# Expert units of the first six batches, run in turn with the last batch's remaining work

## The chip, the cores and the metric

The kernel runs on one core of a Trainium2 chip. The metric is the device time of one execution in microseconds (us). Its engines are TensorE (PE, matmuls), VectorE (DVE), ScalarE (ACT), GpSimd (POOL) and SyncE (SP). POOL and SP issue the transfers of the part in question: POOL the indirect ones, that is scatters and accumulating scatters, SP the plain ones and the transposing ones.

## The reference, cut to what matters

```python
x = x + tanh(g_xattn) * attention(layernorm(x), ctx)        # x: 8 batches x 512 tokens x 512; 8 heads of 64
h = layernorm(x)
logits = h @ gate_w                                        # 8 experts
topv, topi = top_k(logits, 2);  w = softmax(topv)
Y[e] = (silu(h @ Wu[e]) * (h @ Wv[e])) @ Wo[e]             # 512 -> 128 -> 512
x = x + tanh(g_ffn) * sum_k w[k] * Y[topi[k]]
```

There are 4096 tokens with two experts each, so 8192 rows are to be added to the output. On the reference's own inputs the eight experts get 1147, 971, 688, 1113, 1074, 929, 1219 and 1051 rows; after the first six batches it is 848, 753, 417, 770, 821, 688, 1021 and 826.

## The kernel before

**Steps.** The attention goes in 32 steps `g` (batch `b`, pair of heads `j`), each `step(b, j)` being written out in program order on every engine. Tiles of 128 tokens lag behind: in step `g` PE transposes and projects the attention output of tile `n = g - 4` (`("oT", n)`, `("out", n)`), DVE adds it to the residual (`x2_rows`, L874 to L879, with the row's statistics), POOL works out the layernorm factors (`factors2`, L530 to L533), ACT normalises twice (`normalise2`, L697 and L700), POOL splits off the low half (`row_lo`, L542), SP turns the row with a transposing transfer (`turn`, L392), PE forms the logits two steps later. After a batch's four tiles DVE picks the two experts (`best_two`), PE counts ranks, DVE works out each row's place in its expert's list (`places`, done at L945), and POOL scatters the rows into the lists in device memory (`scatter`, L551, two halves of four transfers, each after a small `hold`, L518).

**The tail.** After step 31 a loop over `g = 32 .. 38` does what the last batch still needs: tiles 28 to 31, the logits of 26 to 31, the choices and scatters of batches 6 and 7.

**The table.** Then `unit_table` (DVE, L967 to L1011) cuts the lists into 39 units of 256 rows. An expert's first unit is the ragged last window of its list, pulled back so that it ends with the list (`block_ == 0`); then come blocks 1, 2, ... from the start. The pulled-back window overlaps the last whole block. Rows that would be added twice get weight 0. Units left over repeat the last expert's windows with weight 0.

**The units.** For unit `s` SP loads 256 rows (L497, three buffers), PE transposes them (L1371), multiplies by `Wu` and `Wv` (L1379) and, one unit later, by `Wo` (`down`, L1390); ACT takes tanh (L793), copies the high half (L798) and scales the two result tiles (`results`, L787, four buffers); DVE multiplies (L1147, L1153) and splits (L1157). POOL adds the results to the output with two accumulating indirect transfers of 128 rows (L631). Two such adds may touch the same output row when they belong to different experts or to overlapping windows, so `unit(s)` in POOL's program waits:

```python
if 0 < s < 3:
    pool.wait_ge(added[(s - 1) % 2], 2 * 16)
if s >= 3:
    before = pool.value_load(need[0:1, s:s + 1], min_val=2 * 16, max_val=32 * UNITS)
    pool.wait_ge(added[(s - 1) % 2], before)
hold()
pool.wait_ge(y_taken, K * (s + 1))
since(pool, added[s % 2], s // 2 * 2 * 16)
```

Every unit waits for the adds of unit `s - 2`. It waits for those of `s - 1` as well where `need` says so: where the expert differs from that of `s - 1`, or the window starts less than 256 rows from that of `s - 1` (L1006 to L1011). The general PSUM banks `G` hold both the tail's products and the units' transposed rows. The order on each engine is the program's; nothing is reordered at run time.

Of the kernel before, what the change touches and what calls it, by code (L numbers as in the profile page):

```python
# [11 lines left out]
P = 128  # L12
# [44 lines left out]

def bank_uses(B, TT):
# [27 lines left out]
    for g in range(steps, steps + 6):  # L86
        if g < steps + 4:
            names += [("oT", g - 4), ("out", g - 4)]
        names.append(("logits", g - 6))
        if g % 4 == 1:  # L90
            names.append(("ranks", g // 4 - 2))
# [3 lines left out]
def layer(nc, x, ctx_in, g1, wq, wk, wv, wo, bo, g2, gate_w, wu, wvf, wof, out, C):  # L95
# [18 lines left out]
    UNITS = ROWS * K // UR + E - 1  # L114
    HEAD = 8
# [16 lines left out]
    with ctx:  # L132
# [86 lines left out]
        cum = sb("cum", [P, 4, E])  # L219
# [6 lines left out]
        ue, unit_expert, unit_off, need = (take(UNITS) if k == 0 else take(UNITS).bitcast(U32) for k in range(4))  # L226
        uw = take(7 * UNITS).rearrange("p (k u) -> p k u", k=7)
        ids = take(K * UNITS).bitcast(U32).rearrange("p (u k) -> p u k", k=K)
        valid = take(K * UNITS).rearrange("p (u k) -> p u k", k=K)

        p32 = P32[:].rearrange("p t s -> p (t s)")
        cmp = p32[:, 0:E * BE].rearrange("p (e b) -> p e b", e=E)
        ucmp = p32[:, E * BE:E * BE + UNITS * E].rearrange("p (u e) -> p u e", e=E)
        ucmp2 = p32[:, E * BE + UNITS * E:E * BE + 2 * UNITS * E].rearrange("p (u e) -> p u e", e=E)
        spare = p32[:, E * BE + 2 * UNITS * E:4 * S]
# [77 lines left out]

        table_ready = sem("unit_table_ready")
        need_ready = sem("needed_adds_ready")
# [33 lines left out]
        def _(sp):  # L349
# [126 lines left out]
            for g in range(STEPS, STEPS + 5):  # L476
                if g < STEPS + 4:
                    load_residual(g - 4)
                turn(g - 5)
                if g < STEPS + 4:  # L480
                    store_x2(g - 4)

            sp.wait_ge(table_ready, 2)
            sp.wait_ge(outsider_st, E * K * 16)
            sp.wait_ge(prefix_st, 16)
            for r in range(2):
                for h in range(2):
                    sp.wait_ge(scattered[r][h], B // 2 * 2 * K * 16)

            def unit_rows(s):  # L490
                r = s % XG
                if s >= XG:
                    sp.wait_ge(m_filled, 2 * (s - XG) + 2)
                    sp.wait_ge(w_sel, s - XG + 1)
                    sp.wait_ge(ids_ready, s - XG + 1)
                first = sp.value_load(unit_off[0:1, s:s + 1], min_val=0, max_val=E * REGION - UR)
                sp.dma_start(xg_words[:, r], table[bass.ds(first, UR), :].rearrange("(p k) c -> p k c", k=K)) \  # L497
                    .then_inc(rows_ld[r], 16)

            for s in range(UNITS):  # L500
                unit_rows(s)
            for r in range(2):
                sp.wait_ge(x2_st[r], TILES // 2 * 16)
                sp.wait_ge(added[r], (UNITS + 1 - r) // 2 * 2 * 16)

        @block.gpsimd
        def _(pool):
# [95 lines left out]
            for g in range(STEPS, STEPS + 7):  # L603
                if g < STEPS + 5:
                    factors2(g - 5)
                if g < STEPS + 4:
                    add_bias(g - 4)
                if g < STEPS + 5:
                    row_lo(g - 5)
                if g % 4 == 2:  # L610
                    scatter(g // 4 - 2, 0)
                    scatter(g // 4 - 2, 1)

            for r in range(2):
                pool.wait_ge(x2_st[r], TILES // 2 * 16)

            pool.wait_ge(need_ready, 1)

            def unit(s):

                pool.wait_ge(ids_ready, s + 1)
                if 0 < s < 3:
                    pool.wait_ge(added[(s - 1) % 2], 2 * 16)
                if s >= 3:
                    before = pool.value_load(need[0:1, s:s + 1], min_val=2 * 16, max_val=32 * UNITS)
                    pool.wait_ge(added[(s - 1) % 2], before)
# [3 lines left out]
                for k in range(K):  # L630
                    nc.gpsimd.indirect_dma_start(out_rows, bass.IndirectOffsetOnAxis(ids[:, s, k:k + 1], 0),  # L631
# [3 lines left out]
            for s in range(UNITS):  # L635
                unit(s)

        @block.scalar
        def _(act):
# [129 lines left out]
            for g in range(STEPS, STEPS + 6):  # L769
                if g < STEPS + 4:  # L770
                    hi_part(("oT", g - 4), oT[0][:], 1.0)
                if g < STEPS + 5:
                    normalise2(g - 5)
                if g % 4 == 1:
                    gap_exp(g // 4 - 2)
# [15 lines left out]
            for s in range(UNITS):  # L791
                act.wait_ge(u_filled, s + 1)
# [11 lines left out]
        def _(dve):  # L804
# [156 lines left out]

            def unit_table():

                spread_e = lambda z: z.unsqueeze(1).to_broadcast([P, UNITS, E])
                spread_u = lambda z: z.unsqueeze(2).to_broadcast([P, UNITS, E])
                before, block_, limit, off, over, blocks, flag = (uw[:, k, :] for k in range(7))
# [4 lines left out]
                link(nc.vector.tensor_reduce(cum[:, 0, :], cmp, AXX, ALU.add))  # L971
                for k, d in enumerate((1, 2, 4)):
                    nc.vector.tensor_copy(cum[:, k + 1, 0:d], cum[:, k, 0:d])
                    link(nc.vector.tensor_tensor(cum[:, k + 1, d:E], cum[:, k, d:E], cum[:, k, 0:E - d], ALU.add))
                link(nc.vector.tensor_tensor(ucmp, spread_e(cum[:, 3, :]), spread_u(C["unit_no"][:]), ALU.is_le))
                nc.vector.tensor_reduce(limit, ucmp, AXX, ALU.add)
                link(nc.vector.tensor_tensor(ucmp2, ucmp, spread_e(cum[:, 0, :]), ALU.mult))
                link(nc.vector.tensor_reduce(before, ucmp2, AXX, ALU.add))
                nc.vector.tensor_scalar(ue, limit, float(E - 1), None, ALU.min)
                link(nc.vector.tensor_tensor(block_, C["unit_no"][:], before, ALU.subtract))  # L980

                nc.vector.tensor_copy(unit_expert, ue).then_inc(table_ready, 1)
                nc.vector.tensor_tensor(over, limit, ue, ALU.subtract)
                link(nc.vector.tensor_tensor(ucmp, spread_e(C["iota"][:]), spread_u(ue), ALU.is_equal))
                nc.vector.tensor_scalar(flag, block_, 0.0, None, ALU.is_equal)
                link(nc.vector.tensor_tensor(ucmp2, ucmp, spread_e(cum[:, 0, :]), ALU.mult))
                link(nc.vector.tensor_reduce(blocks, ucmp2, AXX, ALU.add))
                nc.vector.tensor_tensor(ucmp, ucmp, spread_e(nt[:, 1, :]), ALU.mult)
                link(nc.vector.tensor_tensor(blocks, blocks, flag, ALU.mult))
                nc.vector.tensor_reduce(limit, ucmp, AXX, ALU.add)  # L990
                link(nc.vector.tensor_tensor(block_, block_, blocks, ALU.add))
                link(nc.vector.tensor_scalar(block_, block_, -1.0, float(UR), ALU.add, ALU.mult))
                link(nc.vector.tensor_tensor(limit, limit, block_, ALU.min))
                link(nc.vector.scalar_tensor_tensor(out=off, in0=ue, scalar=float(REGION), in1=limit,
                                                    op0=ALU.mult, op1=ALU.add))
                nc.vector.tensor_scalar(unit_off, off, float(UR), None, ALU.add).then_inc(table_ready, 1)
                nc.vector.tensor_tensor(block_, block_, limit, ALU.subtract)

                step_ = flag[:, 0:UNITS - 1]
                link(nc.vector.tensor_tensor(step_, off[:, 1:UNITS], off[:, 0:UNITS - 1], ALU.subtract))  # L1000
# [45 lines left out]
            def step(b, j):  # L1046
# [60 lines left out]
                if g == 9:  # L1107
                    outsiders()
# [384 lines left out]
```

## Time and profile before

| | |
|---|---|
| time, median of 3 runs (lowest to highest) | 1117.78 us (1116.68 to 1119.32) |
| the profiled execution: its time, its span | 1116.96 us, 1115.2 us |
| mean granted TensorE clock | 0.933 of full speed |
| busy: PE, DVE, ACT, POOL | 903.0, 679.0, 572.3, 533.9 us |
| last scatter of batch 5 issued | 796.96 us |
| last scatter of batch 7 issued | 862.23 us |
| first row load of the units | 866.06 us |
| first and last add of the units issued | 884.66 and 1104.87 us |

Times within the span count from its start. The first 800 us are the attention, the next 70 the tail, the rest the units.

### The profile page before, as it was taken

The page shows a single profiled execution, that of the slowest core. Times are in us where ns is not written, and L with a number is a line of the kernel's source. Part 1 is how long each engine was busy: PE and PEld are TensorE (multiplying, and loading weights), DVE is VectorE, ACT ScalarE, POOL GpSimd, SP SyncE. Part 2 cuts the span into 40 slices and gives each one's busy share as a digit, 9 for nine tenths or more (in the row PEclk, how much of TensorE's full clock was granted, in tenths as well). Part 3 has the DMA queues.
Part 4 walks back from the last instruction along what each step waited for, and adds up shares of the span by engine and source line. Part 5 has one row for each costly group of instructions (what it writes and reads, how often), then busy time and mean ns, then how long its engine had stood idle before and what let it go on. Part 6 is the DMA issues. An engine that isn't in the chain of part 4 may idle for free.

```text
span 1115.2 us, 22759 instructions
## 1 busy us (share of the span) xinstructions
PE 903.0 (81%) x8210; PEld 543.6 (49%) x8210; DVE 679.0 (61%) x1596; ACT 572.3 (51%) x1023; POOL 533.9 (48%) x643
## 2 busy tenths in 40 slices
PE   1758898899899899989989989896650799798880
PEld 1314444455455555545545555453320677576660
DVE  3537777767867777776777777488335354344440
ACT  3316665666656655755655664465420365455450
POOL 5003224334447556446635744536564146566664
PEclk9978899999999999999999999899875799999995
DMA  6455573252254336227326434634453588899996
GB/s 225 163 149 175 164 232 115 67 150 71 76 171 112 77 103 187 72 67 204 97 58 183 112 87 140 201 77 118 135 157 103 141 185 180 166 198 188 195 152 83
DMA packets 124285, 154.26 MB, mean 138 GB/s; under 512 B 48272, under 2 KB 81040, under 8 KB 123792
## 3 DMA queue, kind: packets, MB, share of 16 engines
q1 hardware_dynamic: 107312, 115.40, 35.4%
q0 software_dynamic: 16864, 37.40, 17.6%
q8 instruction: 69, 1.13, 0.4%
q14 instruction: 40, 0.33, 0.1%
HBM read 62.83 MB, written 56.30 MB: 107 GB/s over the span
## 4 chain that ended last, share of the span: by engine, by line
PE 50%; DMA 13%; DVE 12%; ACT 8%; issue 8%; POOL 5%; SPq 3%; POOLq 1%; ACTq 0%; DVEq 0%
PE G L1173 25%; DMA out_dram<-V,Ph 9%; PE MX L1213 3%; PE ST L1228 3%; PE ST L1227 3%; PE G L1182 3%; PE MX L1379 2%; PE PV L1240 2%; PE PV L1242 2%; POOL out_dram L631 2%; PE PV L1244 2%; DVE mx L830 2%; SPq L365 2%; POOL expert_rows L551 1%; DVE tiles L820 1%
## 5 line engine op out<-in xcount | busy, mean ns | idle before, releaser
L663 ACT ACTIVATE P<-ST 128x512 f32<-128x512 f32 x256 | 153.1, 598 | 209.4 <-PE ST L1228 205.3
L588 POOL TENSOR_TENSOR Pl<-P,Ph 128x512 f16<-128x512 f32 x128 | 151.6, 1191 | 211.9 <-ACT Ph L666 211.5
L830 DVE TENSOR_REDUCE mx<-MX 128x1 f32<-128x512 f32 x256 | 168.1, 683 | 27.0 <-PE MX L1213 26.6
L666 ACT ACTIVATE Ph<-ST 128x512 f16<-128x512 f32 x256 | 154.1, 602 | 1.0 <-PE PV L1244 0.5
L631 POOL DMA_INDIRECT out_dram<-V,Ph x78 | 122.1, 1566 | 49.4 <-ACT V L787 31.7
L1379 PE MATMUL MX<-heads,tiles 128*128 128x256 f16 x936 | 118.1, 278 | 18.9 <-DVE heads L1127 18.1
L1240 PE MATMUL PV<-V,Ph 128*128 128x65 f16 x1024 | 113.3, 195 | 16.0 <-issue 16.0
L1240 PEld LDWEIGHTS PV<-V,Ph 128*128 128x128 f16 x1024 | 97.4, 98 | 36.5 <-issue 19.0
L1242 PE MATMUL PV<-V,Ph 128*128 128x64 f16 x1024 | 113.5, 197 | 0.0
L1244 PE MATMUL PV<-V,Pl 128*128 128x65 f16 x1024 | 113.1, 194 | 0.0
L1379 PEld LDWEIGHTS MX<-heads,tiles 128*128 x936 | 90.4, 100 | 41.3 <-issue 25.0
L1227 PE MATMUL ST<-heads 128*128 128x512 f16 x256 | 98.8, 386 | 9.9 <-DMA heads<-mrow 7.7
L1242 PEld LDWEIGHTS PV<-V,Ph 128*128 128x128 f16 x1024 | 96.8, 99 | 18.7 <-issue 1.2
L1213 PE MATMUL MX<-heads 128*128 128x512 f16 x256 | 91.9, 392 | 16.4 <-DVE mx L830 13.4
L1228 PE MATMUL ST<-heads 128*128 128x512 f16 x256 | 99.1, 387 | 0.0
L867 DVE TENSOR_TENSOR Pl<-P,Ph 128x512 f16<-128x512 f32 x128 | 97.0, 761 | 2.9 <-ACT Ph L666 2.9
L1244 PEld LDWEIGHTS PV<-V,Pl 128*128 128x128 f16 x1024 | 97.2, 101 | 0.0
L1173 PE MATMUL G<-tiles,wq_hi 128*128 128x512 f16 x256 | 79.8, 395 | 9.3 <-DVE tiles L820 9.3
L1173 PE MATMUL G<-wv_hi,tiles 128*128 128x512 f16 x256 | 83.2, 388 | 3.6 <-DVE V L851 2.1
L1173 PE MATMUL G<-tiles,wk_hi 128*128 128x512 f16 x256 | 76.3, 380 | 0.0
L538 POOL TENSOR_TENSOR second_norm<-second_norm,tgbo 128x512 f32<-128x512 f32 x32 | 42.4, 1325 | 66.0 <-DMA second_norm<-in_x_dram 66.0
L551 POOL DMA_INDIRECT expert_rows<-second_norm,pos_staged x64 | 65.2, 1020 | 17.3 <-issue 17.0
(204 smaller groups left out, 1872.0 us busy)
## 6 DMA issues: line engine op xcount, KB each, us to landing
heads<-expert_rows SPq DMA_DIRECT2D x39, 516.0 KB
tiles<-in_x_dram SPq DMA_DIRECT2D x32, 256.0 KB, 5.1
tiles<-in_ctx_dram SPq DMA_DIRECT2D x32, 256.0 KB, 5.3
heads<-q_hi SPq DMA_DIRECT2D x128, 64.0 KB, 2.0
heads<-k_hi SPq DMA_DIRECT2D x128, 64.0 KB, 2.0
second_norm<-in_x_dram SPq DMA_DIRECT2D x32, 256.0 KB, 3.0
out_dram<-second_norm SPq DMA_DIRECT2D x32, 256.0 KB, 2.3
expert_rows<-Pl SPq DMA_DIRECT2D x1, 4128.0 KB, 16.5
```

The lines of the kernel that those rows point to most:

```text
L588: nc.gpsimd.tensor_tensor(Pl[:, hh, c, :], P32[:, c, :], Ph[:, hh, c, :], ALU.subtract).then_inc(pl_pool, 1)
L631: nc.gpsimd.indirect_dma_start(out_rows, bass.IndirectOffsetOnAxis(ids[:, s, k:k + 1], 0), y_sb[:, s % YR, k, :], None, compute_op=ALU.add) \
L663: nc.scalar.activation(P32[:, c, :], ST[:, c % 2, :], ACT.Exp, scale=0.125 / SC2).then_inc(p_ready, 1)
L666: nc.scalar.activation(Ph[:, hh, c, :], ST[:, c % 2, :], ACT.Exp, scale=0.125 / SC2).then_inc(ph_ready, 1)
L830: nc.vector.tensor_reduce(out=mx[:, k // TT, k % TT:k % TT + 1], in_=MX[:, (k + odd) % 2, :], axis=AXX, op=ALU.max).then_inc(mx_taken, 1)
L1173: last = nc.tensor.matmul(out_, a, m, start=(n == 0), stop=(n == len(parts) - 1))
L1227: nc.tensor.matmul(ST[:, c % 2, :], K1[:, j, hh, cols], Q1[:, j, hh, :], start=True, stop=False)
L1228: nc.tensor.matmul(ST[:, c % 2, :], K2[:, j, hh, cols], Q2[:, j, hh, :], start=False, stop=True).then_inc(st_filled, 1)
L1240: nc.tensor.matmul(out_[:, 0:HD + 1], Ph[:, hh, c, cols], V[:, r, c, h, 0:HD + 1], start=(c == 0), stop=False)
L1242: nc.tensor.matmul(out_[:, 0:HD], Ph[:, hh, c, cols], V[:, r, c, h, HD + 1:], start=False, stop=False)
L1244: last = nc.tensor.matmul(out_[:, 0:HD + 1], Pl[:, hh, c, cols], V[:, r, c, h, 0:HD + 1], start=False, stop=(c == TT - 1))
L1379: last = nc.tensor.matmul(dst, w, uT[:, s % 2, a, c * UR:(c + 1) * UR], start=k == 0, stop=k == len(parts) - 1)
```

## The change

The 39 units are split in 17 early ones and 22 late ones. 17 is the number of whole blocks of 256 rows that six batches fill whatever the routing is: (6144 - 8 x 255) / 256, rounded up. A second table, `early_table`, is made by DVE at the end of step 30 from the list lengths that six batches give; it takes each expert's whole blocks in order until it has 17, and keeps in `used` how many of each expert it took. The late table (`unit_table`) takes what is left of each list: the ragged last window first, then the whole blocks after the `used` ones. The early units start once the last scores are done (their row buffers lie over the heads' operands) and batch 5 is scattered. The loop of the tail is gone; its parts stand in eight gaps `between(v)` in front of units 0 to 7 (on POOL: in front of the adds of unit `v - 1`, with the scatters of batches 6 and 7 in gaps 3 and 8). SP loads rows three units ahead, each after its gap. Unit 17 waits on POOL for the adds of unit 16 without asking the table.

```diff
+GAPS = 8
+def tail_uses(v, first):
+    names = []
+    if 1 <= v <= 4:
+        names.append(("out", first + v - 1))
+    if v <= 3:
+        names.append(("oT", first + v))
+    if v in (0, 1, 3, 4, 5, 6):
+        names.append(("logits", first - 2 + v if v < 2 else first - 3 + v))
+    if v in (2, 7):
+        names.append(("ranks", first // 4 - (v == 2)))
+    return names
...
+    EARLY_BATCHES = B - 2
+    EARLY = -(-(EARLY_BATCHES * S * K - E * (UR - 1)) // UR)
+    LATE = UNITS - EARLY
...
@@ block.sync
+            load_residual(TILES - TT)
+            sp.wait_ge(early_ready, 3)
+            sp.wait_ge(st_filled, STEPS * 8)
+            for r in range(2):
+                for h in range(2):
+                    sp.wait_ge(scattered[r][h], EARLY_BATCHES // 2 * 2 * K * 16)
+            for s in range(XG):
+                unit_rows(s)
             for s in range(UNITS):
-                unit_rows(s)
+                if s < GAPS:
+                    between(s)
+                if s + XG == EARLY:
+                    sp.wait_ge(table_ready, 3)
...
+                if s + XG < UNITS:
+                    unit_rows(s + XG)
@@ block.gpsimd
+            def between(v):
+                n = TILES - TT + v
+                if v == 0:
+                    factors2(n - 1)
+                if 2 <= v <= 5:
+                    factors2(n - 2)
+                if v < 4:
+                    add_bias(n)
+                if v == 0:
+                    row_lo(n - 1)
+                if 2 <= v <= 5:
+                    row_lo(n - 2)
+                if v in (3, 8):
+                    scatter(B - 2 + v // 8, 0)
+                    scatter(B - 2 + v // 8, 1)
...
+                if s and (s < 3 or s == EARLY):
+                    pool.wait_ge(added[(s - 1) % 2], ((s - 1) // 2 + 1) * 2 * 16)
+                elif s:
+                    wanted = pool.value_load(listed(e_need, l_need, s)[0:1], min_val=2 * 16, max_val=32 * UNITS)
+                    pool.wait_ge(added[(s - 1) % 2], wanted)
...
+            for v in range(UNITS + 1):
+                if v <= GAPS:
+                    between(v)
+                if v == EARLY:
+                    pool.wait_ge(table_ready, 3)
+                if v:
+                    unit_add(v - 1)
@@ block.scalar
+            def between(v):
+                n = TILES - TT + v
+                if v < 4:
+                    hi_part(("oT", n), oT[0][:], 1.0)
+                if v == 0:
+                    normalise2(n - 1)
+                if 2 <= v <= 5:
+                    normalise2(n - 2)
+                if v in (1, 6):
+                    gap_exp(B - 2 + v // 6)
@@ block.vector, unit_table
-                link(nc.vector.tensor_reduce(cum[:, 0, :], cmp, AXX, ALU.add))
+                link(nc.vector.tensor_reduce(cum[:, 4, :], cmp, AXX, ALU.add))
+                link(nc.vector.tensor_tensor(cum[:, 0, :], cum[:, 4, :], used, ALU.subtract))
...
+                link(nc.vector.tensor_tensor(ucmp2, ucmp, spread_e(used), ALU.mult))
+                nc.vector.tensor_reduce(done, ucmp2, AXX, ALU.add)
...
+                link(nc.vector.tensor_tensor(block_, block_, done, ALU.add))
@@ block.vector
+                if g == STEPS - 2:
+                    early_table()
...
+                if 1 <= v <= 4:
+                    x2_rows(n - 1)
+                if v < 4:
+                    lo_part(("oT", n), oT[1][:], oT[0][:], 1.0)
...
+                if v == 7:
+                    unit_table()
@@ block.tensor
+                if units_turned.value:
+                    pe.wait_ge(t_lo if u % 2 else t_hi, units_turned.value)
...
+                pe.wait_ge(evacuated, use["oT", TILES - TT] if s == 0 else 1 + max(
+                    use[name] for v in range(min(s, GAPS)) for name in tail_uses(v, TILES - TT)))
```

On POOL, before, the scatters of batch 7 (`expert_rows`) end the tail and the adds (`out_dram`) come behind them, each behind its `junk` hold:

```order
L518 TENSOR_TENSOR junk<-ones 128x1
L551 DMA expert_rows<-second_norm,pos_staged 34944x516 x4
L518 TENSOR_TENSOR junk<-ones 128x1
L551 DMA expert_rows<-second_norm,pos_staged 34944x516 x4
L518 TENSOR_TENSOR junk<-ones 128x1
L631 DMA out_dram<-V,Ph 4096x512 x2
L518 TENSOR_TENSOR junk<-ones 128x1
L631 DMA out_dram<-V,Ph 4096x512 x2
```

On POOL now, the end of gap 3, with the scatters of batch 6, stands between the adds of unit 1 and unit 2, and the factors of tile 30 stand behind unit 2's adds:

```order
L586 TENSOR_TENSOR second_norm<-second_norm,tgbo 128x512
L590 TENSOR_TENSOR second_norm<-second_norm 128x512
L566 TENSOR_TENSOR junk<-ones 128x1
L599 DMA expert_rows<-second_norm,pos_staged 34944x516 x4
L566 TENSOR_TENSOR junk<-ones 128x1
L599 DMA expert_rows<-second_norm,pos_staged 34944x516 x4
L566 TENSOR_TENSOR junk<-ones 128x1
L682 DMA out_dram<-V,xn 4096x512 x2
L578 TENSOR_SCALAR ln_factors<-row_mean_var 128x1
L579 TENSOR_TENSOR ln_factors<-ln_factors,ln_constants 128x1
L580 TENSOR_SCALAR ln_factors<-ln_factors 128x1
L581 TENSOR_SCALAR ln_factors<-row_mean_var,ln_factors 128x1
```

What moved: adds, scatters and the factors of the last tiles share POOL's program in turn, where before every factor and scatter stood ahead of the first add.

On DVE now, the late table (43 instructions, of which the first four and the last two are shown) stands in gap 7, between the places of batch 7 and unit 7's first product (`P<-P,MX`):

```order
L1007 CAST pos_staged<-pos_f 128x8
L1035 TENSOR_TENSOR nt<-base,list_starts 128x8
L1036 TENSOR_SCALAR nt<-nt 128x8
L1037 TENSOR_TENSOR P<-nt,block_starts 128x128
L1039 TENSOR_REDUCE cum<-P 128x8
...
L1080 TENSOR_TENSOR Ph<-Ph 128x21
L1081 SCALAR_TENSOR_TENSOR Ph<-Ph,adds_before 128x21
L1262 SCALAR_TENSOR_TENSOR P<-P,MX 128x256
L1234 COPY heads<-G 128x1024
```

Before (39 instructions), on DVE, it had the same place behind the places of batch 7, and unit 0's turned rows (`heads<-G`) came next:

```order
L945 CAST pos_staged<-pos_f 128x8
L967 TENSOR_TENSOR nt<-base,list_starts 128x8
L968 TENSOR_SCALAR nt<-nt 128x8
...
L1010 TENSOR_TENSOR Ph<-Ph 128x38
L1011 SCALAR_TENSOR_TENSOR Ph<-Ph,adds_before 128x38
L1127 COPY heads<-G 128x1024
```

What moved: the table stood ahead of all units; now seven units are ahead of it.

## Rows read from the trace of the kernel before

**Rows 1.** The page: the span, and its part on transfers issued (residual tiles)

```profile
span 1115.2 us, 22759 instructions
...
second_norm<-in_x_dram SPq DMA_DIRECT2D x32, 256.0 KB, 3.0
```

**Rows 2.** Windows: us; PE, PEld, DVE, ACT, POOL busy; clock, DMA share, GB/s

```profile
801.50:872.50 71.00, 24.15 (x219) 13.41 (x215) 27.26 (x127) 11.19 (x17) 33.20 (x47) 0.65 0.40 127
...
884.00:990.00 106.00, 97.26 (x907) 76.29 (x906) 49.78 (x176) 57.54 (x98) 57.24 (x51) 0.97 0.87 182
```

**Rows 3.** Timeline of POOL: first adds of units 0, 2, 5, 17, 31, 35, 36, 38

```profile
884.66 1.62 POOL L631 DMA_INDIRECT out_dram<-V,Ph  x1 [11.72 <-ACT V L787]
...
903.37 1.57 POOL L631 DMA_INDIRECT out_dram<-V,Ph  x1 [0.39 <-ACT V L787]
...
922.11 1.56 POOL L631 DMA_INDIRECT out_dram<-V,Ph  x1 [0.50 <-issue]
...
990.25 1.56 POOL L631 DMA_INDIRECT out_dram<-V,Ph  x1 [0.50 <-issue]
...
1069.79 1.56 POOL L631 DMA_INDIRECT out_dram<-V,Ph  x1 [0.50 <-ACT V L787]
...
1087.22 1.56 POOL L631 DMA_INDIRECT out_dram<-V,Ph  x1 [1.43 <-ACT V L787]
...
1095.13 1.56 POOL L631 DMA_INDIRECT out_dram<-V,Ph  x1 [0.50 <-issue]
...
1103.01 1.56 POOL L631 DMA_INDIRECT out_dram<-V,Ph  x1 [0.40 <-issue]
```

**Rows 4.** Waits, 866 to the end: who waited for whom, total, times, longest

```profile
POOL junk L518 <- DMA out_dram<-V,Ph: 43.0, 8, 6.5
```

**Rows 5.** Transfers that write the output: issue to landing

```profile
DMA to landing us min/median/max: 2.0/5.3/8.5
```

**Rows 6.** The chain that ended last: pieces of one unit on PE

```profile
883.54 1.31 PE MX L1379 x12
884.85 0.89 PE G L1371 x16
...
887.05 1.29 PE PV L1390 x6
```

**Rows 7.** Timeline of POOL: last scatter of batch 5; batch 6's scatter; bias

```profile
796.96 0.96 POOL L551 DMA_INDIRECT expert_rows<-second_norm,pos_staged  x1 [0.30 <-issue]
...
823.12 0.19 POOL L518 TENSOR_TENSOR junk<-ones 128x1 f32<-128x1 f32 x1
...
833.60 0.25 POOL L530 TENSOR_SCALAR ln_factors<-row_mean_var 128x1 f32<-128x1 f32 x1
...
835.15 1.27 POOL L538 TENSOR_TENSOR second_norm<-second_norm,tgbo 128x512 f32<-128x512 f32 x1
```

**Rows 8.** Timeline of SP's queue: the first five row loads

```profile
866.06 15.96 SPq L497 DMA_DIRECT2D heads<-expert_rows  x5
```

**Rows 9.** Timeline of ACT: second normalisation of tile 30; unit 1's tanh; unit 0's results

```profile
835.95 0.80 ACT L700 ACTIVATE second_norm<-second_norm,ln_factors 128x512 f16<-128x512 f32 x1
...
880.08 0.39 ACT L793 ACTIVATE P<-MX 128x256 f32<-128x256 f32 x1 [0.36 <-PE MX L1379]
...
883.14 1.25 ACT L787 ACTIVATE V<-ST,unit_scales 128x512 f32<-128x512 f32 x2
```

**Rows 10.** Timeline of DVE: first and last instruction of the table

```profile
851.98 0.16 DVE L967 TENSOR_TENSOR nt<-base,list_starts 128x8 f32<-128x8 f32 x1
...
861.71 0.20 DVE L1011 SCALAR_TENSOR_TENSOR Ph<-Ph,adds_before 128x38 uint32<-128x38 f32 x1
```

**Rows 11.** Windows of 5 us where PE idled; columns as in rows 2

```profile
970.00:975.00 5.00, 0.35 (x3) 0.24 (x3) 1.51 (x4) 2.59 (x5) 2.56 (x4) 0.82 0.81 109
975.00:980.00 5.00, 5.00 (x33) 4.02 (x32) 2.20 (x8) 2.85 (x5) 4.54 (x5) 0.50 1.05 215
...
1025.00:1030.00 5.00, 1.90 (x12) 0.87 (x10) 1.51 (x4) 2.73 (x5) 3.94 (x4) 1.00 1.05 145
```

More of the change, by code:

```diff
@@ L85, in bank_uses @@
         names += second
[L86 to L91, printed above, removed]
+    for v in range(GAPS):
+        names += tail_uses(v, steps - 4)
     return names
@@ L602, in _, with unit_add @@
                     step(b, j)
[L603 to L619, printed above, removed]
-                pool.wait_ge(ids_ready, s + 1)
[L622 to L626, printed above, removed]
+            def between(v):
[13 more added lines that the diff above has]
+                    scatter(B - 2 + v // 8, 1)
+            def unit_add(s):
+                pool.wait_ge(ids_ready, s + 1)
+                if s in (0, EARLY):
+                    for r in range(2):
+                        pool.wait_ge(x2_st[r], (EARLY_BATCHES * TT if s == 0 else TILES) // 2 * 16)
+                if s and (s < 3 or s == EARLY):
[3 more added lines that the diff above has]
+                    pool.wait_ge(added[(s - 1) % 2], wanted)
                 hold()
@@ L768, in _, with between @@
                     step(b, j)
[L769 to L775, printed above, removed]
+            def between(v):
+                n = TILES - TT + v
+                if v < 4:
+                    hi_part(("oT", n), oT[0][:], 1.0)
+                if v == 0:
+                    normalise2(n - 1)
+                if 2 <= v <= 5:
+                    normalise2(n - 2)
+                if v in (1, 6):
+                    gap_exp(B - 2 + v // 6)
             def unit_hi(s):
@@ L791, in _ @@
             for s in range(UNITS):
+                if s < GAPS:
+                    between(s)
                 act.wait_ge(u_filled, s + 1)
@@ L1145, in _ @@
             for s in range(UNITS):
+                if s < GAPS:
+                    between(s)
                 dve.wait_ge(tanh_ready, s + 1)
@@ L1162, in _ @@
         def _(pe):
+            units_turned = Count(0)
             def bank(name):
@@ L1355, in _, with between @@
             pe.wait_ge(o_ready, B * HB)
-            for g in range(STEPS, STEPS + 6):
-                if g < STEPS + 4:
-                    transposes(("oT", g - 4), O[(B - 1) % 2][:, g - STEPS, :])
-                    out_project(g - 4)
-                logits(g - 6)
-                if g % 4 == 1:
-                    ranks(g // 4 - 2)
+            def between(v):
+                for name in tail_uses(v, TILES - TT):
+                    what, n = name
+                    if what == "out":
+                        out_project(n)
+                    elif what == "oT":
+                        transposes(name, O[(B - 1) % 2][:, v, :])
+                    elif what == "logits":
+                        logits(n)
+                    else:
+                        ranks(n)
             def unit_transposes(s):
                 r = s % XG
+                units_turned.take()
                 pe.wait_ge(rows_ld[r], (s // XG + 1) * 16)
+                pe.wait_ge(evacuated, use["oT", TILES - TT] if s == 0 else 1 + max(
+                    use[name] for v in range(min(s, GAPS)) for name in tail_uses(v, TILES - TT)))
                 for a, taken in ((0, t_hi), (1, t_lo)):
@@ L1403, in _ @@
             for s in range(UNITS):
+                if s < GAPS:
+                    between(s)
                 pe.wait_ge(t_hi, s + 1)
```

190 lines of the change are left out of this document (119 added, 71 removed).

## The prediction

> **What bounds the kernel now.** I read the windows first. After the last head PE works 24.15 of 71 us up to the units, at a clock of 0.65 [rows 2]: that is the slack which the change is about. In the units PE works 97.26 of 106 us and the transfers show 0.87 [rows 2]. One unit is, on PE, 0.89 us of transposes, twice 1.31 for `Wu` and `Wv` and 1.29 for `Wo` [rows 6]: 4.8 us. But from unit 17 to unit 31, 14 units, the adds take 1069.79 - 990.25 = 79.5 us [rows 3], 5.7 us each. What takes the rest shows in the waits: eight times POOL's hold in front of an add stands until the previous unit's adds have landed, 43.0 us in all [rows 4]. With lists of 1147, 971, 688, 1113, 1074, 929, 1219 and 1051 rows the experts have 5, 4, 3, 5, 5, 4, 5 and 5 units, 36; their changes fall on units 5, 9, 12, 17, 22, 26 and 31, and unit 36, the first spare one, repeats the ragged window beside the block that it overlaps. These are eight waits, and the count agrees. Units 1 and 2 wait by the program.
>
> What such a wait costs: units 0 to 2 are two waited intervals, (903.37 - 884.66) / 2 = 9.36 us each; from unit 35 to 36, with no row load left, it is 1095.13 - 1087.22 = 7.91. An interval without it is (1103.01 - 1095.13) / 2 = 3.94, POOL's own pace [rows 3]. PE runs ahead meanwhile, by up to four result buffers, so one wait among five units costs little. Waits in a row are another matter: then a unit costs 8 to 9 us, whatever PE does.
>
> **The change, part by part.** I follow the time of the adds.
>
> *Start.* Before, 3.8 us passed from the last scatter's issue at 862.23 to the first row load at 866.06 [rows 8]. The last scatter of batch 5 is issued at 796.96 [rows 7], so the first load comes at 800.8, 65 us earlier. The first add came 884.66 - 866.06 = 18.6 us behind the load. Gaps 0 and 1 now stand in it (a projection, two turned tiles, two logits, a choice of experts), of which some 4 us are not hidden: first add near 823.5.
>
> *Early table.* Some 23 small DVE instructions; the table of before has 39 in 861.71 + 0.20 - 851.98 = 9.9 us [rows 10], so these are about 5.5 us, behind step 30. I cost them at nothing: scores and exponentials of step 31 cover them, and uncovered they cost 5.5.
>
> *Gaps 2 to 7.* Each is a round through POOL, ACT, DVE and PE. When ACT ends unit v-2's results, POOL issues their adds (3.8 us, above), then works out the factors of the next tile, on which ACT's two normalisations wait: from 833.60 [rows 7] to 835.95 + 0.80 = 836.75 [rows 9], 3.15 us for both. ACT's tanh of unit v stands behind them; from a tanh to the end of the previous unit's results it is 883.14 + 1.25 - 880.08 = 4.3 us [rows 9]. The sum is 11.2 us a round. PE's own work in it (4.8, and near 4 of projection, turning and logits) is hidden.
> - Gaps 2 and 5: 11.2 each.
> - Gaps 3 and 4: between them POOL has adds 3.8, factors and normalisation 3.15, the residual's load 3.0 [rows 1], its bias 1.27 [rows 7] and a low half of about as much, then batch 6's scatters from 823.12 to 833.60, 10.5 us [rows 7], adds 3.8, factors and normalisation 3.15, and 4.3. Sum 34.
> - Gap 6: no factors, but the last turned row and the choice of two experts; 7.5, an estimate between 4.3 and 11.2.
> - Gap 7: places (some 2 us), the late table (43 narrower instructions, 9.9 as before), then 4.3: 16.
> - Sum 80. Unit 6's adds come at 823.5 + 80 = 903.5. Batch 7's scatters stand ahead of unit 7's: + 3.8 + 10.5 = 917.8.
>
> *Early units 7 to 17.* The early list (3, 2, 1, 3, 3, 2, 3 blocks of experts 0 to 6) changes expert at 9, 12 and 14, and 17 waits always. A group of three with its wait is 922.11 - 903.37 = 18.7 us [rows 3]; one of two is a waited 9.4 and an unwaited 3.9 to 4.3, so 13.5. Unit 17: 917.8 + 13.5 + 18.7 + 13.5 + 18.7 = 982. Before it is 990.25 [rows 3]. Of a head start of 65 us, 8 are left.
>
> *Late units.* The early table took all whole blocks but the last from most lists. What is left of the eight is 2, 2, 2, 2, 2, 2, 2 and 5 units. In every pair the first is the ragged window, pulled back, the second the last whole block, which it overlaps: 891 and 768 for expert 0, 715 and 512 for expert 1, and so on, always less than 256 apart. So `need` asks for the previous adds at the change of expert and again inside the pair: all 14 intervals from unit 17 to unit 31 are waited ones, where before three were. Before, the overlapping blocks stood three to four units apart and needed nothing of this. Each interval lies between 7.91 (no row loads beside the adds) and 9.36 (nearly two loads beside each, since PE ran at 4.8). With one load beside each I take 8.7. That is 122 us in place of 79.5: unit 31 at 1104.
>
> By the Trainium skill (DMA: Bandwidth & Descriptors, "Anatomy of one DMA") a transfer costs about 2.0 us and its bytes at 436 GB/s; an add of 256 KB would be back 2.6 us after its issue. The interval would then be some 5.2 us (half of POOL's 3.94 up to the second transfer, 2.6, and the hold), and the 14 waits would cost nothing; the rows show 7.91 where the adds are alone, so I weigh it only as a rival.
>
> *End.* Unit 31 begins a group of five, as before; from there to the end 1115.2 - 1069.79 = 45.4 us [rows 1, 3] stay.
>
> Sum of the span: 1104 + 45.4 = 1149.4, 34 above 1115.2. The profiled execution took 1116.96, 1.8 above its span, and the median is 0.8 above that: 1152; with gaps that may overlap a little better than in my sum I say 1151.
>
> **Rivals.**
> 1. *The adds' waits are short when the queue is empty, and the kernel is faster.* The place is the 14 intervals from unit 17 to 31. It decides at (1069.79 - 982) / 14 = 6.3 us an interval. For it: the shortest landing of such a transfer is 2.0 us [rows 5]; then POOL's own pace of 3.94 and PE's 4.8 bound an interval, and the total 982 + 67 + 45.4 + 2.6 = 1097. Against it: the median is 5.3 [rows 5], and the interval with no load beside it is 7.91. The skill's figure above gives 5.2 an interval, so 1103. Chance 0.05.
> 2. *PE falls to its lower clock in the gaps and the late units, and becomes the bound.* After a stretch with 0.35 us of work in 5 PE's clock is 0.50 for the next 5, that is 1.2 GHz in place of 2.4; after one with 1.90 of 5 it stays at 1.00 [rows 11]. Late units leave PE 8.7 - 4.8 = 3.9 us idle each, between the two. At 1.2 GHz a unit is 9.6 us of PE, 0.9 over the interval: 13 us over 14; a gap is near 17.6 against 11.2, up to 25 over four. Half of the whole gives 1170. Chance 0.13. [...]
> 3. *The gaps cost little and the late waits alone count.* If ACT does not wait for POOL's factors, a round is some 6 us, unit 17 comes near 965 (the waited groups catch up with it in part), and the total is near 1133. Chance 0.12; against it stands ACT's program order.
> 4. *No difference:* the head start and the waits cancel. That is the band around rival 1's point. Chance 0.02.
>
> **How the numbers follow.** Forecast 0.68, rivals 0.05, 0.13, 0.12, 0.02. A measurement here can tell 0.2% (2.2 us) from nothing. Bounds of the forecast: late intervals 7.91 or 9.36, -11 or +9; gaps 10 either way. That is 1130 to 1170; the range goes a little beyond on both sides for rivals 2 and 3: 1128 to 1174. Faster 0.05, same 0.02, slower 0.93.
>
> **What would show it.** In the profile after: first add of the output near 823, unit 17's near 982; POOL's holds in front of adds waiting on the output's transfers some 20 times instead of 8, above 80 us in all; 14 intervals of 8 to 9 us from unit 17 on; PE busy about 4.8 of each, transfers' share well under 0.87 there; ACT waiting for the factors in gaps 2 to 5. I am wrong if intervals of waited adds fall under 6.3 us, or if the start of the units slips behind 830.

## The result, and the profile after

The changed kernel takes 1153.17 us (median of 4 runs, 1151.42 to 1158.87), where the kernel before takes 1118.55 us (4 runs, 1116.68 to 1121.18). The ratio is 1.0316, 95% interval 1.0289 to 1.0343: slower by 34.6 us. The forecast was 1151. The profiled execution took 1152.34 us, with a span of 1150.5. All ratios in this document compare fast runs; one execution of the kernel before, taken beside experiments 5 to 8, was slow (2078.95 us) and is left out of them.

I read the profile after in the order of the forecast's steps. First POOL's timeline, first adds of units 0, 1, 3, 6, 7, 17 and 31. The columns are start, duration, line and operation, and in brackets how long POOL had idled before it and what ended that.

```profile
823.32 1.67 POOL L682 DMA_INDIRECT out_dram<-V,xn  x1 [3.52 <-ACT V L847]
...
835.62 1.65 POOL L682 DMA_INDIRECT out_dram<-V,xn  x1 [0.18 <-issue]
...
869.66 1.66 POOL L682 DMA_INDIRECT out_dram<-V,xn  x1 [2.16 <-ACT V L847]
...
904.02 1.56 POOL L682 DMA_INDIRECT out_dram<-V,xn  x1 [5.93 <-ACT V L847]
...
918.24 1.83 POOL L682 DMA_INDIRECT out_dram<-V,xn  x1 [0.16 <-POOL junk L566]
...
982.00 1.55 POOL L682 DMA_INDIRECT out_dram<-V,Ph  x1 [0.52 <-ACT V L847]
...
1105.73 1.55 POOL L682 DMA_INDIRECT out_dram<-V,Ph  x1 [0.50 <-ACT V L847]
```

Against [rows 3] the first add comes 61.3 us earlier (823.32, before 884.66), unit 17's 8.3 us earlier (982.00, before 990.25), and unit 31's 35.9 us later (1105.73, before 1069.79). So the head start is lost in two places. From the first add to unit 17, 158.7 us pass in place of 105.6: 53 us given back, 48.6 of them up to unit 7, that is in the gaps (94.9 in place of 46.3), and 4.4 between units 7 and 17. From unit 17 to unit 31, 123.7 in place of 79.5: 44 us more than before. Behind unit 31 nothing changed: 1150.5 - 1105.73 = 44.8, before 45.4 [rows 1, 3].

The waits from 800 us to the end (who waited for whom; us in total, times, longest), the four lines that the forecast spoke of:

```profile
POOL junk L566 <- DMA out_dram<-V,Ph: 70.2, 15, 5.6
...
ACT second_norm L754 <- POOL ln_factors L581: 30.5, 4, 15.8
...
POOL junk L566 <- DMA out_dram<-V,xn: 29.3, 6, 6.2
...
ACT P L855 <- PE MX L1505: 10.3, 12, 2.1
```

POOL's hold in front of an add waits for the adds of the unit before 21 times and 99.5 us; before it was 8 times and 43.0 us [rows 4]. (`V,xn` and `V,Ph` are the same result buffers; the early and the late table lie in different memory.) ACT waits for PE's `Wu` products (`MX`), with which each unit begins on ACT, for no more than 10.3 us in all: PE is not what the late units wait for.

The windows: first the old tail's, then the gaps, the early units 7 to 17, and the 14 late intervals. The columns are those of [rows 2].

```profile
801.50:872.50 71.00, 44.23 (x403) 31.14 (x404) 27.79 (x95) 22.64 (x37) 33.58 (x41) 0.83 0.58 146
823.00:903.00 80.00, 44.74 (x410) 31.88 (x409) 34.83 (x149) 23.94 (x41) 41.16 (x50) 0.83 0.59 136
903.00:982.00 79.00, 71.86 (x657) 56.37 (x655) 35.04 (x122) 41.53 (x72) 45.14 (x44) 0.96 0.85 193
982.00:1105.73 123.73, 85.43 (x678) 63.82 (x674) 34.14 (x126) 39.98 (x71) 46.04 (x43) 0.89 0.59 122
```

The change does what it says: in the 71 us that were the tail, PE works 44.2 us in place of 24.15 [rows 2], with units between the rest of the last batch. But the last window shows the price. No engine is busy there for more than 85 of 124 us, the transfers' share is 0.59 where units without such waits in a row had 0.87 [rows 2], and each unit takes 8.84 us.

One late interval in POOL's timeline:

```profile
990.64 1.55 POOL L682 DMA_INDIRECT out_dram<-V,Ph  x1 [0.50 <-ACT V L847]
992.50 1.55 POOL L682 DMA_INDIRECT out_dram<-V,Ph  x1 [0.30 <-issue]
998.28 0.19 POOL L566 TENSOR_TENSOR junk<-ones 128x1 f32<-128x1 f32 x1 [4.23 <-DMA out_dram<-V,Ph]
998.96 1.56 POOL L682 DMA_INDIRECT out_dram<-V,Ph  x1 [0.50 <-ACT V L847]
```

Two issues with 0.30 between them end 3.41 us after the first began. Then POOL stands for 4.23 us until the second add has landed, 998.28 - 992.50 = 5.8 us after its issue began. With the hold's 0.19 and 0.49 to the next issue that is 8.32 us.

### The profile page after: what moved, and what is told of

Same layout as the page of the kernel before. It is cut to its first block, busy times and chain, and to the rows that moved or that the text cites. A ratio compares the mean times of both kernels' runs of the same rounds, so it can differ in the third digit from the quotient of the medians.

```text
span 1150.5 us, 22775 instructions
## 1 busy us (share of the span) xinstructions
PE 914.2 (79%) x8210; PEld 552.9 (48%) x8210; DVE 679.4 (59%) x1606; ACT 571.8 (50%) x1023; POOL 531.6 (46%) x643
## 3 DMA queue, kind: packets, MB, share of 16 engines
q0 software_dynamic: 16864, 37.40, 16.7%
## 4 chain that ended last, share of the span: by engine, by line
PE 45%; DMA 14%; DVE 11%; issue 10%; ACT 8%; POOL 8%; SPq 3%; POOLq 1%; ACTq 0%; DVEq 0%
PE G L1292 24%; DMA out_dram<-V,Ph 8%; POOL out_dram L682 4%; PE MX L1332 3%; PE ST L1347 3%; PE ST L1346 3%; PE G L1301 3%; DMA out_dram<-V,xn 2%; PE PV L1361 2%; PE PV L1363 2%; PE PV L1359 2%; ACT V L847 2%; POOL expert_rows L599 2%; DVE mx L892 2%; SPq L400 2%
## 5 line engine op out<-in xcount | busy, mean ns | idle before, releaser
L1505 PE MATMUL MX<-heads,tiles 128*128 128x256 f16 x936 | 129.8, 295 | 58.7 <-DVE heads L1234 58.7
L1505 PEld LDWEIGHTS MX<-heads,tiles 128*128 x936 | 94.5, 105 | 85.7 <-issue 68.0
L1347 PE MATMUL ST<-heads 128*128 128x512 f16 x256 | 99.5, 389 | 0.0
L929 DVE TENSOR_TENSOR Pl<-P,Ph 128x512 f16<-128x512 f32 x128 | 92.6, 727 | 0.0
L682 POOL DMA_INDIRECT out_dram<-V,Ph x44 | 68.2, 1550 | 17.6 <-ACT V L847 9.7
```

The lines of the kernel that those rows point to most:

```text
L1347: nc.tensor.matmul(ST[:, c % 2, :], K2[:, j, hh, cols], Q2[:, j, hh, :], start=False, stop=True).then_inc(st_filled, 1)
L1505: last = nc.tensor.matmul(dst, w, uT[:, s % 2, a, c * UR:(c + 1) * UR], start=k == 0, stop=k == len(parts) - 1)
```

## The experiments

The first four kernels were run on one chip (kernel before there: 1127.57 us, 7 runs, 1123.54 to 1129.86), the last four on another (kernel before there: 1127.19, 14 runs, 1119.86 to 1130.29). On both, positions within a span are some 8 to 13 us later than in the runs above, from the first add on. I compare ratios and intervals between units.

**Theory A** is the forecast's: the 14 late intervals cost 8.7 to 8.8 us each because each unit waits for the adds of the one before, and the gaps cost 80 us because POOL's work stands in one row. **Theory B** is that the waits are only where the lateness shows: the late units would be about as slow without them, for PE's lower clock or the short groups' other costs. **Theory C** is that, in the gaps, ACT's wait for POOL's layernorm factors is the bound, not the scatters.

### 1. The waits alone, in the kernel before

```diff
-                if 0 < s < 3:
-                    pool.wait_ge(added[(s - 1) % 2], 2 * 16)
-                if s >= 3:
+                if 0 < s < 3 or 17 < s <= 31:
+                    pool.wait_ge(added[(s - 1) % 2], ((s - 1) // 2 + 1) * 2 * 16)
+                elif s >= 3:
```

> The kernel before, whose POOL program waits at each of units 18 to 31 for the adds of the unit just before, by constants; nothing else is changed. If waits in a row are what the late units pay for (my theory), units 17 to 31 take 14 x 8.8 = 123 us in place of 79.5, and the time is near 1118 + 44 = 1162 us (1155 to 1168). If such waits are cheap and the changed kernel loses its time elsewhere (PE at its lower clock, the gaps), it stays within 1118 to 1130.

Measured: 1173.81 us, ratio 1.043 (1.0405 to 1.0455). Units 17 to 31 took from 999.90 to 1121.86, so 8.71 us an interval. In the window over these 14 intervals:

```profile
999.90:1121.86 121.96, 82.98 (x654) 61.32 (x652) 33.99 (x126) 40.27 (x71) 46.45 (x42) 0.90 0.58 122
```

This is the row of the changed kernel's late units (0.89, 0.59, 122 GB/s) in a kernel that has the old table, the old tail and the old order. The waits are sufficient for the whole slowness of that stretch, and B's "short groups" play no part. The kernel lost 46.2 us by the medians; in its profiled execution, which at 1169.0 us was the fastest of five, units 17 to 31 took 42.5 us more than before (121.96 in place of 79.5).

### 2 and 3. The late units with and without their waits

Whether a late unit may go without waiting depends on the rows it adds to. So two kernels send the late units' adds to rows of their own (and so leave the sums of units 18 to 38 out of the result):

```diff
+                    c = s % (ROWS // 256) * 2 + k
+                    rows_ = C["rows_of"][:, c:c + 1] if s > EARLY else ids_of(s)[:, k:k + 1]
-                    nc.gpsimd.indirect_dma_start(out_rows, bass.IndirectOffsetOnAxis(ids_of(s)[:, k:k + 1], 0),
+                    nc.gpsimd.indirect_dma_start(out_rows, bass.IndirectOffsetOnAxis(rows_, 0),
```

The second of them drops the wait for unit `s - 1` behind unit 18:

```diff
-                elif s:
+                elif 0 < s <= EARLY + 1:
```

With the waits:

> The changed kernel, whose units 18 to 38 add their results to 256 rows of their own each (a constant list of row numbers, block s mod 16 of the output) in place of their tokens' rows; their sums are thus left out of the result. All waits stay. It is the control for the next run: if where the adds go does not matter, 1153 us as the changed kernel (1148 to 1158). If scattered rows cost the adds something, it is faster than that by itself.

Measured: 1165.88 us, ratio 1.034 (1.0302 to 1.0379), as the changed kernel (1.0316); units 18 to 31 took 1122.61 - 1007.71 = 114.9, 8.84 an interval. Where the rows lie makes no difference beyond these intervals.

Without them:

> As the run before (units 18 to 38 add to rows of their own, their sums are left out), and units 19 to 38 do not wait for the unit just before them, whose rows are others now; each still waits for the last but one. My theory: units 17 to 31 fall from 8.8 us each to the pace of PE and the transfers, 5.3, so 50 us less, and unit 36's wait goes too: 1100 us (1092 to 1110). If the transfers themselves or a slow PE clock set the pace of the late units, they stay above 7 us each and the time above 1130.

Measured: 1111.64 us, ratio 0.9862 (0.9839 to 0.9886). Units 18 to 31 took 1067.61 - 1003.01 = 64.6, 4.97 an interval. The two windows over units 18 to 31, with the waits and then without:

```profile
1007.71:1122.61 114.90, 77.72 (x598) 57.37 (x598) 31.56 (x117) 37.27 (x66) 42.74 (x39) 0.87 0.58 120
```

```profile
1003.01:1067.61 64.60, 58.17 (x537) 44.91 (x538) 29.69 (x108) 34.69 (x62) 43.34 (x40) 0.97 0.99 196
```

B falls. With the waits gone and everything else in place, 13 intervals are 50.3 us shorter, and the kernel 0.048 x 1127.57 = 54 us. PE's clock rises from 0.87 to 0.97 by itself: the lower clock was a result of the idling. What is left at 4.97 us is the work of PE and the transfers (PE 58.17 of 64.60, share 0.99). The kernel without the waits is also 1.4% faster than before. That is not the worth of the overlap alone: this kernel also does without the waits at units 22, 26, 31 and 36, which the kernel before has, and those cannot be left out where the sums have to be right. Experiment 8 has the overlap with the sums right.

### 4. The scatters moved

In gaps 3 and 8 all eight scatters of a batch stand in front of adds whose results are ready. Here the two halves of batch 6's stand behind the factors in gaps 2 and 3, where ACT is normalising, and batch 7's in gap 7, ahead of unit 6's adds:

```diff
                 if 2 <= v <= 5:
                     factors2(n - 2)
+                if v in (2, 3):
+                    scatter(B - 2, v - 2)
...
-                if v in (3, 8):
-                    scatter(B - 2 + v // 8, 0)
-                    scatter(B - 2 + v // 8, 1)
+                if v == 7:
+                    scatter(B - 1, 0)
+                    scatter(B - 1, 1)
```

> The changed kernel with the scatters of batch 6 and 7 earlier in POOL's program: batch 6's halves behind the factors of gaps 2 and 3, where POOL waits for the residual anyway, and batch 7's in front of unit 6's adds, where POOL waits for DVE's table. My sum of the gaps: 10.5 us come off ACT's wait in gap 4, and 10.5 off the way from unit 6's adds to unit 7's. Unit 6 adds at 894 in place of 904, unit 17 at 962 in place of 982, and the late units stay at 8.8 each: 1133 us (1127 to 1141). If the waits among units 7 to 17 give it back, unit 17 stays above 972 and the time above 1143.

Measured: 1149.55 us, ratio 1.0198 (1.0172 to 1.0225). POOL's timeline in gap 7:

```profile
905.61 0.96 POOL L599 DMA_INDIRECT expert_rows<-second_norm,pos_staged  x1 [0.30 <-issue]
906.60 0.20 POOL L566 TENSOR_TENSOR junk<-ones 128x1 f32<-128x1 f32 x1
907.08 1.62 POOL L684 DMA_INDIRECT out_dram<-V,xn  x1 [0.28 <-issue]
909.00 1.56 POOL L684 DMA_INDIRECT out_dram<-V,xn  x1 [0.30 <-issue]
910.02 0.77 POOL L566 TENSOR_TENSOR junk<-ones 128x1 f32<-128x1 f32 x1
913.78 1.56 POOL L684 DMA_INDIRECT out_dram<-V,xn  x1 [2.99 <-ACT V L849]
```

From unit 0 to unit 6: 907.08 - 833.13 = 73.95 us, on the same chip 81.75 in experiment 2, which has the gaps of the changed kernel. From unit 6 to 7: 6.7 in place of 14.2. Together 15.3 us of the 21 expected. The scatters stood on the path where they were in front of ready adds. What is missing of the 21 is, for the most part, not their cost in the new place. In gap 7 they end 0.5 us before unit 6's adds, yet units 5 to 6 took 14.4 us, in experiment 2 14.3. But without them in front of unit 7's adds POOL waited 2.99 us for ACT's results there (the last line above), which is the 3 us missing at that unit. In front of unit 2's adds, too, POOL now waited for ACT, 1.22 us, and units 1 to 2 took 14.4 us in place of 23.2.

### 5. Factors ahead of the adds

Theory C's test, on top of experiment 4's edit: in gaps 2 to 8 the adds go one gap later, so that POOL works out the factors before it issues adds, and ACT need not wait behind them.

```diff
-                if v == EARLY:
+                if v == min(EARLY, GAPS + 1):
                     pool.wait_ge(table_ready, 3)
-                if v:
+                if 2 <= v <= GAPS:
+                    unit_add(v - 2)
+                if v == GAPS + 1:
+                    unit_add(v - 2)
+                if v > GAPS:
                     unit_add(v - 1)
```

> The run with the scatters moved, and on POOL the adds of a unit stand one gap later in gaps 2 to 8, behind the factors on which ACT waits. My sum had the adds' 3.8 us inside each round; taken out, gaps 4 and 5 have factors 1.6, normalisation 1.5, low half 1.2 and adds 3.8 on POOL, 8 us in place of 10.5; gaps 2 and 3 are POOL's own 12.3 us (the residual's load and bias stand in them) and stay. So 4 us less than with the scatters moved alone, a ratio of 1.016 to the kernel before (1.011 to 1.020). If ACT's wait on the factors is not what sets a gap, no difference, 1.020.

Measured: 1150.17 us, ratio 1.0193 (1.0158 to 1.0229), against experiment 4's 1.0198 on the other chip (each against the kernel before on its own): no difference that can be told. The waits of this kernel from 800 us on:

```profile
POOL junk L566 <- DVE pos_staged L1013: 16.7, 2, 9.0
ACT second_norm L760 <- POOL ln_factors L581: 12.0, 3, 7.8
```

ACT's wait for the factors did fall, from 21.6 us in experiment 4 to 12.0. In its place POOL's first scatters of a batch now wait 16.7 us for DVE's places, and the adds stand behind them. C is not the bound by itself: with the factors early, the next thing in the row is late.

### 6. One whole block less per expert in the early list

If the waits of pairs are the price, the late groups should be longer. The early list here takes only whole blocks up to the last but one (9 early units), so that late groups have 3, 3, 3, 3, 3, 3, 4 and 5 units, the ragged window being two units from the block that it overlaps:

```diff
-    EARLY = -(-(EARLY_BATCHES * S * K - E * (UR - 1)) // UR)
+    EARLY = -(-(EARLY_BATCHES * S * K - E * (2 * UR - 1)) // UR)
...
-                link(nc.vector.tensor_scalar(nt[:, 0, :], nt[:, 0, :], float(-UR), None, ALU.add))
+                link(nc.vector.tensor_scalar(nt[:, 0, :], nt[:, 0, :], float(-2 * UR), None, ALU.add))
```

> The changed kernel, whose early table leaves one whole block more of every list to the late units: 9 early units (2, 1, 0, 2, 2, 1, 1, 0 of the experts) and 30 late ones in groups of 3, 3, 3, 3, 3, 3, 4 and 5, so that a ragged window and the block that it overlaps never stand side by side. Late units waiting for the unit before: 9 in place of 16. But unit 9's rows wait for batch 7's scatters in gap 8. My sum: unit 9 adds some 5 us later than in the changed kernel, then 6 groups of 18.7, one of 22.5, one of 25 and the end of 20: ratio 1.002 to the kernel before (0.993 to 1.012). If the late units cost 8.8 us whatever they wait for, 1.03 and more.

Measured: 1140.01 us, ratio 1.0115 (1.007 to 1.016). The holds' waits fell from 21 and 99.5 us to 11 and 59.0. But unit 7's adds came 939.00 - 911.97 = 27.0 us behind unit 6's, not 14.2. The timelines of SP, PE and ACT show it:

```profile
928.59 11.67 SPq L518 DMA_DIRECT2D heads<-expert_rows  x4
...
932.13 1.89 PE L1497 MATMUL G<-identity,heads 128*128 128x128 f16 x16 [19.43 <-DMA heads<-expert_rows]
...
933.21 1.02 ACT L839 ACTIVATE heads<-G 128x1024 f16<-128x1024 f16 x1 [20.08 <-PE G L1497]
...
937.47 1.25 ACT L847 ACTIVATE V<-PV,unit_scales 128x512 f32<-128x512 f32 x2
```

Unit 9 is now the first late one. SP loads its rows only when batch 7's scatters have landed, and POOL issues those behind unit 6's adds, until 925.8. PE turns rows two units ahead, so unit 9's missing rows stop PE and ACT (19.4 and 20.1 us) in front of unit 7's results. The 12.8 us over the 14.2 are enough for the whole miss: 1.0115 - 1.002 is 10.7 us.

### 7 and 8. The same, with the scatters moved, and the factors first

Both edits were tried again on top of experiment 6. With the scatters moved as in experiment 4:

> Both: one whole block less per list in the early table, and the scatters moved. Batch 7's scatters no longer stand behind unit 6's adds, so unit 9's rows come 15 to 18 us earlier; the groups are those of the run before. Ratio 0.986 to the kernel before (0.978 to 0.995): this one should beat both kernels. If the two gains overlap (both in front of unit 9), it is no better than 0.998.

Measured: 1122.26 us, ratio 0.9964 (0.9933 to 0.9995). Unit 7 follows unit 6 after 921.95 - 908.34 = 13.6 us in place of 27.0, since the rows of unit 9 come earlier. Unit 9 itself adds at 940.54, 17.9 us earlier than in experiment 6, and the kernel gained 1.5% on that one, where the two expectations lie 1.6% apart. POOL at units 6 and 7:

```profile
908.34 1.62 POOL L684 DMA_INDIRECT out_dram<-V,xn  x1 [0.93 <-ACT V L849]
...
918.39 0.19 POOL L566 TENSOR_TENSOR junk<-ones 128x1 f32<-128x1 f32 x1 [6.56 <-DMA out_dram<-V,xn]
921.95 1.56 POOL L684 DMA_INDIRECT out_dram<-V,xn  x1 [3.38 <-ACT V L849]
```

With the adds one gap later as well:

> The run before with the factors in front of the adds as well. If the gaps set the time of unit 9, 4 us less than the run before: ratio 0.982 (0.974 to 0.990). If the late groups set everything once unit 9 is there, the same gain, since unit 9 comes earlier; only if the adds' delay by one gap is paid at unit 9 is there none.

Measured: 1117.85 us, ratio 0.9919 (0.9893 to 0.9946), 0.8% faster than the kernel before and the fastest here of those that compute the whole output. Its waits:

```profile
POOL junk L566 <- DMA out_dram<-V,Ph: 42.9, 8, 7.0
POOL junk L566 <- DMA out_dram<-V,xn: 21.5, 4, 7.8
ACT second_norm L760 <- POOL ln_factors L581: 13.0, 3, 7.8
POOL junk L566 <- DVE pos_staged L1013: 11.1, 2, 7.1
PE G L1503 <- DMA heads<-expert_rows: 10.6, 2, 6.6
```

Both came out slower than expected, by 1.0% or some 11 us. It was not the late groups: units 9 to 36 took 161.0 and 159.4 us, and the sum of experiment 6 had 6 x 18.7 + 22.5 + 25 = 159.7. The loss lies in front of them. Units 6 to 9 took 32.2 us in experiment 7 and 31.0 in experiment 8, where with 17 early units they took 21.2 (experiment 4) and 17.7 (experiment 5). The rows of the first late unit are still late (PE waits 10.6 us here for rows, 9.5 in experiment 7), but they do not stand alone. With only 9 early units, unit 7 and unit 8 each begin another expert, so each must wait for the adds before it. In front of unit 7 POOL's hold stood 6.56 us in experiment 7 (the lines above) and 7.81 in experiment 8, and only behind that did POOL wait for ACT's results, 3.38 and 0.83 us. So rows in time would have brought unit 7 forward by no more than about that. In front of unit 8 the hold stood 3.95 and 4.76 us. The shorter early list took waits out of the late groups and put two of them here.

Why "factors first" gave 5 us here and nothing in experiment 5 is not settled: the intervals of 7 and 8 overlap, and DVE's places held POOL for 11.1 us here and 16.7 there.

## Why the prediction was right

| step | forecast | measured |
|---|---|---|
| first add | 823.5 | 823.32 |
| unit 0 to 1 (gap 2) | 11.2 | 12.3 |
| unit 1 to 3 (gaps 3, 4) | 34 | 34.0 |
| unit 3 to 4 (gap 5) | 11.2 | 10.3 |
| unit 4 to 5 (gap 6) | 7.5 | 10.3 |
| unit 5 to 6 (gap 7) | 16 | 13.8 |
| sum of the gaps | 80 | 80.7 |
| unit 6 to 7 (batch 7's scatters) | 14.3 | 14.2 |
| unit 7 to 17 | 64 | 63.8 |
| 14 late intervals | 122 (8.7 each) | 123.7 (8.84) |
| behind unit 31 | 45.4 | 44.8 |

**The start.** The early table was costed at nothing. It stands on DVE from 774.58 to 781.33, and batch 5's last scatter was issued at 795.00, not later than before (796.96 [rows 7]).

**The gaps.** The sum was right to 1 us, and two of its terms less so: gap 6 was 2.8 us longer and gap 7 2.2 us shorter than said. They cancel, which was luck. POOL's timeline shows two waits that the sum did not have, the one in gap 2, the other in gap 6:

```profile
832.91 1.27 POOL L586 TENSOR_TENSOR second_norm<-second_norm,tgbo 128x512 f32<-128x512 f32 x1 [4.36 <-DMA second_norm<-in_x_dram]
...
889.21 0.19 POOL L566 TENSOR_TENSOR junk<-ones 128x1 f32<-128x1 f32 x1 [5.73 <-DMA out_dram<-V,xn]
```

In gap 2 POOL stood 4.36 us for the residual's load, which the sum counted only once, at 3.0, in gaps 3 and 4 (there it was 5.22). So gap 2's 12.3 us are POOL's own row of work, with ACT's results ready 2.3 us before their adds were issued, and not the round through ACT that gave 11.2. In gap 6 unit 5's adds waited 5.73 us for those of unit 4 to land: the early list (3, 2, 1, ...) changes expert at units 3, 5 and 6 too, and the prediction named only the changes behind unit 7. That wait ended at 889.4, and ACT's results for unit 5 came at the same time (888.16 + 1.25), so the round through ACT was longer than 7.5 us as well, and it stays open what gap 6 would be without either. At unit 6 the hold stood 4.16 us, and then POOL waited 5.93 more for ACT.

Experiment 4 confirms the scatters' term: most of it went when they were moved. The round through POOL, ACT, DVE and PE in turn fits units 2 to 3 and 3 to 4 (10.3 us each) and ACT's 30.5 us of waiting for factors, of which 15.8 stand behind batch 6's scatters. But experiment 5 shows that shortening ACT's waits alone brings nothing, so no single one of these waits is shown to be the cause, and how the gaps' 80 us divide among them stays in part argued.

**The late units.** This is where the kernel lost more than the head start left over, and it is shown from both sides: added to the kernel before, the waits give 8.71 us an interval (experiment 1); taken from the late units they leave 4.97 (experiment 3). The value chosen between the bounds 7.91 and 9.36 was 8.7, and 8.84 came.

**Where it was off.** "PE busy about 4.8 of each" was wrong as a sign: PE was busy 85.43 / 14 = 6.1 us. Six of the 14 intervals, and their clocks, show why:

```profile
990.64:998.96 8.32, 4.98 (x46) 3.75 (x46) 2.43 (x9) 2.87 (x7) 3.28 (x3) 1.00 0.62 127
...
1026.46:1034.58 8.12, 6.01 (x44) 4.75 (x45) 2.43 (x9) 2.88 (x7) 3.29 (x4) 0.79 0.62 130
...
1042.98:1052.57 9.59, 6.63 (x46) 4.99 (x46) 2.43 (x9) 2.88 (x6) 3.29 (x4) 0.82 0.59 111
...
1061.58:1069.81 8.23, 4.98 (x46) 3.73 (x46) 2.43 (x9) 2.87 (x6) 3.29 (x4) 1.00 0.61 128
...
1086.41:1096.08 9.67, 4.98 (x46) 3.73 (x46) 2.43 (x9) 2.86 (x6) 3.28 (x3) 1.00 0.53 110
1096.08:1105.73 9.65, 7.54 (x46) 5.55 (x46) 2.43 (x9) 2.88 (x7) 3.29 (x4) 0.65 0.54 111
```

At clock 1.00 a unit is mostly 4.98 us of PE (5.60 at most behind the first), near what was said; in seven of the 14 the mean clock lay between 0.65 and 0.82, that is part of the interval ran at 1.2 GHz in place of 2.4, and the unit took up to 7.54. The interval's length does not follow: 9.67 us with PE at 4.98, 8.12 with PE at 6.01. The mean is 8.71 in the seven at 1.00 and 8.96 in the seven below. So half of rival 2 came true, the clock, and not the other half, that PE becomes the bound: even 7.54 lies under the interval.

**The other rivals.** Rival 1 (short landings) is out: no late interval is near 6.3 us. The adds' transfers took 4.5 to 7.8 us from issue to landing, with a median of 5.7. The estimate of 2.6 us from the figure of the Trainium skill (DMA: Bandwidth & Descriptors, "Anatomy of one DMA") holds for no accumulating transfer seen here. The prediction also gave this rival more than the rows did: the "shortest landing of such a transfer", 2.0 us [rows 5], is that of a plain write of SP to the same tensor. POOL's adds alone took 4.6 us at least in the kernel before, with a median of 6.2 (the first of the two lines in the last section). Rival 3 (cheap gaps) is out by the gaps' 80.7 us. Rival 4 would have needed late intervals of some 6.3 us as well.

## What to carry to other kernels

- Where consecutive items may need each other's results to have landed, count how many such pairs stand in a row, not how many there are. Before, three among 14 units left 5.7 us a unit, against 4.97 where none waits (experiment 3), since PE ran ahead in between; 14 in a row cost 44 us more. Taking the unconflicted work forward is what put the conflicted work in a row: the early list took the blocks that had kept the overlapping ones apart.
- Work that fills an idle stretch is worth only what reaches the queue behind it. PE gained 20 us of work in the old tail, but 53 of the 61 us of head start were given back before unit 17, nearly all in the gaps, where adds, factors, loads and scatters follow each other on POOL. Place each transfer of the gap where its issuing engine would wait anyway, and expect not quite its whole length, since the next wait in the row then shows: 15.3 of 21 us in experiment 4.
- When the first late item is moved forward, ask what its loads wait for and how far ahead the consumer turns to it. In experiment 6 rows missing for unit 9 held up unit 7.

## What the runs showed of the hardware

- With the transfers' share down from 0.87 to 0.59, an add's landing got hardly shorter. Of the adds alone the view of POOL's transfers says, before and then after:

```profile
DMA to landing us min/median/max: 4.6/6.2/8.5
```

```profile
DMA to landing us min/median/max: 4.5/5.7/7.8
```

  These are all adds of either kernel; in the late window alone (982 to 1106 us) the median is 5.7 too (4.8 to 7.1). This suggests that a waited add pays mostly a latency of its own, and little for standing beside other transfers; no run tested it.
- The 14 late intervals are alike in work (PE 44 to 49 matmuls, DVE 9 and ACT 6 or 7 instructions in all but the first) and yet fall in two kinds, 8.1 to 8.6 and 9.0 to 9.7 us, without order and without regard to PE's clock. The difference is in the hold's wait (4.0 to 4.6, or 4.9 to 5.6 us), so in the landing. What makes it was not tried.
